# Self-attention of a transformer block on one core: value products issued for two key tiles at a time, with eight buffers for the exponentials instead of four

## The reference

```python
h = _layernorm(x, ln1_g, ln1_b)
x = _attention(h, h, sa_wq, sa_wk, sa_wv, sa_wo, sa_bo) + x
h = _layernorm(x, ln2_g, ln2_b)
x = _attention(h, cond_emb, ca_wq, ca_wk, ca_wv, ca_wo, ca_bo) + x
h = _layernorm(x, ln3_g, ln3_b)
...
# in _attention
attn = jnp.einsum('bihd,bjhd->bhij', q, k) * scale
attn = jax.nn.softmax(attn, axis=-1)
out = jnp.einsum('bhij,bjhd->bihd', attn, v).reshape(B, S, D_ATTN)
return out @ wo + bo
```

## Time and profile before

| | us |
|---|---|
| median of 3 runs (lowest, highest) | 1568.81 (1566.72, 1576.96) |
| span of the profiled execution | 1578.7 |
| TensorE busy | 1469.8 (93%) |
| VectorE busy | 979.5 (62%) |
| ScalarE busy | 858.7 (54%) |
| GpSimd busy | 923.3 (58%) |

### The profile page before, as it was taken

The page is one execution under the profiler, slowest core; times in us unless marked ns, Lnnn a source line. Parts: engine busy times, 40 slices in busy tenths (PEclk is TensorE's granted clock), DMA queues, the critical chain, the costliest instruction groups (busy, mean ns, idle before and its releaser), DMA issues.

```text
span 1578.7 us, 21167 instructions
## 1 busy us (share of the span) xinstructions
PE 1469.8 (93%) x5921; PEld 821.4 (52%) x5921; DVE 979.5 (62%) x1311; ACT 858.7 (54%) x1498; POOL 923.3 (58%) x513
## 2 busy tenths in 40 slices
PE   5589999999999999999999998689999999968998
PEld 3344555555555555555555543344555555426776
DVE  6457766766776676677667643536777777744333
ACT  4346565565655656565565643546666667535333
POOL 6026767757766775776677687436667777553000
PEclk9689999999999999999999998869999999979999
DMA  2000000000000000000000000200000000000000
GB/s 70 11 14 14 13 2 14 15 0 13 13 1 13 13 13 0 13 13 0 13 14 3 1 13 0 88 20 18 24 24 24 12 24 24 7 1 0 14 13 27
DMA packets 35737, 24.07 MB, mean 15 GB/s; under 512 B 2845, under 2 KB 35443, under 8 KB 35443
## 3 DMA queue, kind: packets, MB, share of 16 engines
q1 hardware_dynamic: 35699, 23.60, 4.9%
HBM read 21.23 MB, written 2.10 MB: 15 GB/s over the span
## 4 chain that ended last, share of the span: by engine, by line
PE 83%; ACT 6%; DVE 5%; POOL 3%; issue 2%; DMA 0%; ACTq 0%; SPq 0%; DVEq 0%; POOLq 0%
PE psum L582 20%; PE psum L502 13%; PE psum L569 11%; PE psum L546 9%; PE psum L570 8%; PE psum L655 5%; PE psum L591 4%; PE psum L644 3%; PE psum L606 2%; PE psum L608 2%; PE psum L607 2%; ACT probs L950 2%; PE psum L550 1%; PE psum L443 1%; PE psum L529 1%
## 5 line engine op out<-in xcount | busy, mean ns | idle before, releaser
L1083 POOL TENSOR_TENSOR acc<-acc,probs 128x1024 f32<-128x1024 f32 x192 | 458.2, 2386 | 184.3 <-ACT probs L950 175.1
L950 ACT ACTIVATE probs<-psum 128x512 f32<-128x512 f32 (+1 forms) x640 | 368.1, 594 | 256.9 <-PE psum L570 234.5
L767 DVE TENSOR_REDUCE m_part<-psum 128x1 f32<-128x512 f32 x512 | 344.9, 687 | 113.0 <-PE psum L546 108.7
L582 PE MATMUL psum<-probs,val 128*64 128x512 f32 (+1 forms) x1280 | 340.8, 620 | 0.2 <-ACT probs L950 0.2
L784 DVE RECIPROCAL recip<-psum 128x512 f32<-128x512 f32 x64 | 214.9, 3358 | 79.0 <-PE psum L591 79.0
L1083 POOL TENSOR_TENSOR acc<-probs 128x1024 f32<-128x1024 f32 (+1 forms) x64 | 152.7, 2386 | 120.1 <-ACT probs L950 71.0
L569 PE MATMUL psum<-qq,self_keys_hh 128*128 128x512 f32 x512 | 219.3, 428 | 2.2 <-ACT probs L950 2.1
L546 PE MATMUL psum<-self_keys_hh,qq 128*128 128x512 f32 x512 | 210.5, 431 | 6.1 <-DVE qq L761 2.8
L570 PE MATMUL psum<-qm,self_keys_lm 128*128 128x512 f32 x512 | 202.9, 396 | 0.0
L569 PEld LDWEIGHTS psum<-qq,self_keys_hh 128*128 128x128 f32 x512 | 96.7, 189 | 121.5 <-ACT probs L950 56.6
L546 PEld LDWEIGHTS psum<-self_keys_hh,qq 128*128 128x128 f32 x512 | 96.1, 190 | 117.5 <-DVE m_part L767 60.6
(11 more groups left out here) (122 smaller groups left out, 2165.5 us busy)
## 6 DMA issues: line engine op xcount, KB each, us to landing
w_raw<-in_L_xattn_ff_w SPq DMA_DIRECT2D x3, 1024.0 KB, 6.8
x_in<-in_x SPq DMA_DIRECT2D x4, 512.0 KB, 4.2
w_raw<-in_L_xattn_sa_wq SPq DMA_DIRECT2D x16, 128.0 KB, 2.1
w_raw<-in_L_xattn_sa_wk SPq DMA_DIRECT2D x16, 128.0 KB, 2.3
w_raw<-in_L_xattn_sa_wv SPq DMA_DIRECT2D x16, 128.0 KB, 2.4
qm<-m_rows SPq DMA_DIRECT2D x128, 2.0 KB
wo_raw<-in_L_xattn_sa_wo SPq DMA_DIRECT2D x16, 128.0 KB, 2.1
w_raw<-in_L_xattn_ca_wq SPq DMA_DIRECT2D x16, 128.0 KB, 2.3
```

What stands on the lines that cost most here:

```text
L582: mm = pe.matmul(psum[d, PV + half % plan.pv_banks, :], val[b][0:plan.ks, kt, d], probs[a % 4][0:plan.ks, h, :], start=(kt == 0), stop=(kt ...
L767: dve.tensor_reduce(m_part[:, half, h, t, kh:kh + 1], psum[:, PV + plan.pv_banks + a % plan.mx_banks, :], AX.X, ALU.max).then_inc(S["x_rea ...
L950: act.activation(probs[u % 4][0:plan.ks, h, :], psum[0:plan.ks, SC + h, :], ACT.Exp, scale=SCALE).then_inc(S["exp_done"], 1)
L1083: pool.tensor_tensor(total, last if kt == 1 else total, now, ALU.add).then_inc(S["acc_done"], 1)
```

## The change

The string for TensorE is written in another order; those of the other engines stay as they are. `P13- P14-`, `P2 P3`, `P4 P5`, `P6 P7`, `P8 P9` and `P10 P11` now stand next to each other, where another step stood between them before; `P15- P0 P1` stood together already, and `P12` stays alone. `P2`, `P4`, `P6` and `P8` move down to the place of the following product, `P13-` and `P10` move down by one step. The buffers `probs` become eight for the self-attention (four of them are used by the cross-attention, as before), and ScalarE's waits for a free buffer reach back eight units instead of four.

```diff
+PROBS = 8
...
-    "pe": "S0.0 S0.1 K0+ P13- S1.0 P14- S1.1 D1- K1+ S2.0 S2.1 P15- P0 P1 S3.0 Q0+ S3.1 S4.0 P2 S4.1 S5.0 "
+    "pe": "S0.0 S0.1 K0+ S1.0 P13- P14- S1.1 D1- K1+ S2.0 S2.1 P15- P0 P1 S3.0 Q0+ S3.1 S4.0 S4.1 S5.0 X0+ Q1+ "
...
+        self.probs = PROBS if own else 4
...
-        probs = [sb(f"probs{b}", [P, 2, HALF], F32, late) for b in range(4)]
+        probs = [sb(f"probs{b}", [P, 2, HALF], F32, late) for b in range(PROBS)]
...
-                                mm = pe.matmul(psum[d, PV + half % plan.pv_banks, :], val[b][0:plan.ks, kt, d], probs[a % 4][0:plan.ks, h, :],
+                                mm = pe.matmul(psum[d, PV + half % plan.pv_banks, :], val[b][0:plan.ks, kt, d], probs[a % plan.probs][0:plan.ks, h, :],
...
-                                after(act, S["pv_done"], plan.units * J + u - 3)
-                                pair, back = (J, u - 4) if u >= 4 else (J - 1, u - 4 + plan.units)
+                                after(act, S["pv_done"], plan.units * J + u - plan.probs + 1)
+                                pair, back = (J, u - plan.probs) if u >= plan.probs else (J - 1, u - plan.probs + plan.units)
                                 after(act, S["acc_done"], 2 * (plan.kt - 1) * pair + plan.added(back))
```

More of the change, by code:

```diff
@@ L944, in emit @@
                             if h == 0:
-                                after(act, S["pv_done"], plan.units * J + u - 3)
-                                pair, back = (J, u - 4) if u >= 4 else (J - 1, u - 4 + plan.units)
+                                after(act, S["pv_done"], plan.units * J + u - plan.probs + 1)
+                                pair, back = (J, u - plan.probs) if u >= plan.probs else (J - 1, u - plan.probs + plan.units)
                                 after(act, S["acc_done"], 2 * (plan.kt - 1) * pair + plan.added(back))
                             act.wait_ge(S["s_ready"], 2 * plan.units * J + 2 * u + h + 1)
-                            act.activation(probs[u % 4][0:plan.ks, h, :], psum[0:plan.ks, SC + h, :], ACT.Exp,
+                            act.activation(probs[u % plan.probs][0:plan.ks, h, :], psum[0:plan.ks, SC + h, :], ACT.Exp,
                                            scale=SCALE).then_inc(S["exp_done"], 1)
@@ L1074, in emit @@
                                 continue
-                            now, last = probs[u % 4][0:plan.ks], probs[(u - 1) % 4][0:plan.ks]
+                            now, last = probs[u % plan.probs][0:plan.ks], probs[(u - 1) % plan.probs][0:plan.ks]
                             total = acc[half][0:plan.ks]
```

## The result

The changed kernel takes 1593.15 us (median of 4 runs, 1590.89 to 1601.55) against 1570.01 us of the kernel before (1566.72 to 1576.96): ratio 1.014, 95% interval 1.0096 to 1.0183. It is slower, by 23 us in the medians; forecast were 21.

What follows compares the result with a forecast made beforehand. TensorE's own sequence was taken to bound the kernel; six moved products sum to +1.47 us per body, 22 us over fifteen bodies, less 1 for buffers, so 1568.8 + 21 = 1590 us, range 1568 to 1598.

Steps and rivals of the forecast that it cites:

- The bound: TensorE is busy throughout a self-attention body, so a body takes what its TensorE steps take, back to back.
- A join is worth 0.34 us: A lone product costs 1.20 us, each beyond the first in a group 0.86; changing the tiling mode drains TensorE.
- P2: Moved to P3: S4.1 waits 1.12 us for exponential S3.1, so nothing is saved; net +0.86 us per body.
- P6 and P8: Moved to P7 and P9: VectorE's reductions hold X12, X13, X24, X25; net +0.67 and +0.47 us per body.
- P4: Moved to P5: V1 waits for ScalarE's copy of V0, gaining 0.71 and costing 0.86; net +0.15 us per body.
- P10 and P13-: Each moves past one step, X29 or S1.0, and uncovers no wait; net -0.34 us each per body.
- The buffers: Eight buffers save 1 us (0 to 3), in the last body; ScalarE's 9.7 us of buffer waits lie in first and last.
- The sum: +1.47 us per body over fifteen bodies is 22, less 1 for the buffers: +21 us, giving 1590 us.
- The whole gain of the joins: Rival: no waits arise at P2, P4, P6, P8, so all six joins win 31 us, giving 1538; chance 0.09.
- VectorE catches up: Rival: P6 and P8 become plain joins, -0.35 us per body, -5 us, giving 1563; chance 0.22.
- The clock: Rival: TensorE's short pauses drop its clock to 1.2 GHz for 6 us per body, giving 1635; chance 0.04.
- slower by over 1%: Outcome above 1584.5 us: 0.55 from the forecast, with the clock rival 0.59.

Runs made afterwards that it cites:

- p10_p13_alone: Kernel before, four buffers, with only P10 moved down to P11 and P13- to P14-; 1569.09 us, ratio 0.9953 to the kernel before.
- four_joins: Kernel before, four buffers, with P13- P14- D1- together and D0 P10 P11 together (D are sums), X30+ before S14.0; 1551.48 us, ratio 0.9855.
- q_split: Changed kernel with the self-attention's copy of the second head of Q moved from ScalarE to VectorE; 1591.5 us, ratio 1.0112 to the kernel before.
- p2_alone: Kernel before with eight buffers and only P2 moved down to P3; 1592.78 us, ratio 1.0097 to the kernel before.
- buffers8: Kernel before with eight buffers instead of four, TensorE's order unchanged; 1575.67 us, ratio 0.9982 to the kernel before.
- order4: Changed kernel's order with four buffers instead of eight; 1592.64 us, ratio 1.0104 to the kernel before.
- p6_p8_alone: Kernel before with eight buffers, only P6 moved down to P7 and P8 down to P9; 1595.51 us, ratio 1.0109 to the kernel before.

## Why the prediction was right

**The bound.** That TensorE's own sequence is the time of a body held: every body length above follows from the starts of TensorE's steps.

**A join is worth 0.34 us.** Shown alone by p10_p13_alone (-0.69 for two) and by four_joins (-1.32 for four, two of them with sums instead of products). One rival is left for the cause. The products differ from their neighbours in two ways, 64 columns instead of 128 and plain float32 instead of float32r, and no run changes one of them alone. The trace speaks against the second: the four transposes `T1+` are plain float32 on all 128 columns, and in the changed kernel they and the `X` behind them take 642.19 to 642.85, 0.66 us. The transposes start 0.11 us apart, and 4 x 0.11 and 0.23 for the `X` make 0.67, so nothing comes on top.

```profile
642.19 0.60 PE L531 MATMUL psum<-ident,valT 128*128 128x128 f32 x4
642.54 0.47 PE L548 MATMUL psum<-self_keys_hh,qq 128*128 128x512 f32 x1
642.85 0.39 PE L571 MATMUL psum<-qq,self_keys_hh 128*128 128x512 f32 x1
```

So the 64 columns are the likely reason, as the prediction has it, and not a shown one.

**P2.** Forecast +0.86 per body, measured alone +0.84. The wait before `S4.1` was 1.14 us from start to start, forecast 1.12, and q_split shows that it is ScalarE's copying of `Q0` that sets it.

**P6 and P8.** Forecast +0.67 and +0.47, measured together +1.15. In the change, `X13` starts at 636.08 and `S7.1` 0.34 later, as the two rules taken from the earlier trace rows say; those two numbers (0.06 for the signal, 0.11 for the restart) carry all four places.

**P4.** Forecast +0.15, not run alone. What is left of the whole, 1.43 - 0.84 - 1.15 + 0.69 = +0.13, is its term. The trace of the change says the same: `V1` starts 0.62 us behind `X6` (628.24 to 628.86), forecast 0.63.

**P10 and P13-.** Forecast -0.68, measured -0.69.

**The buffers.** Right that they are worth nothing; the reason given for the first and last body was not. The prediction read the 9.7 us of the earlier trace rows as waits for a free buffer. With eight buffers the same waits are listed with the same lengths (2.5 us in the first body, 4.7 in two in the last), so they were waits for something else, put down to GpSimd by the table. Hence no microsecond came back in the last body.

**The sum.** Forecast +21, of which 22 by fifteen bodies; measured +1.43 x 15 = 21.4 by the same reckoning. The whole self-attention grew by 23.2 us. Of this the thirteen bodies in the middle have 18.5. The last one has 1.1, from its first scores to its last (39.43 to 40.51 us): the prediction took it as untouched by the order and 1 us shorter by the buffers, but `P2` is moved there too, and p2_alone has 40.30. The first two have 3.6, and how much of that is the change is open, as two kernels with the same order differ there by 1.5 (111.9 us before, 110.4 in buffers8).

That 1590 came so near to 1593.15 is in part luck. The 21 us were added to a median of 1568.8; beside the experiments the kernel before took 1577, and the same order (order4) was then 15 us slower and not 23. The body lengths, which don't depend on this, are what the sum can be held to.

**The rivals.** The whole gain of the joins fails at P2, P6 and P8, each for its own wait. That VectorE catches up fails by p6_p8_alone; its reductions at 0.60 us were not in the rows either, for three in 2.16 us are 0.72 each. The clock stays at 1.00 in the bodies with TensorE busy 54.05 of 56 us; the caution of the Trainium skill on short pauses (TensorE: Matmul & The Clock Gate, "A second HAM failure mode: psum-queue depth-cycling") isn't borne out by pauses of 0.2 to 1.0 us here.

The ratio is 1.014, slower by over 1%, to which the prediction gave a chance of 0.59.

## What to carry to other kernels

When an engine is busy all the time in an order written by hand, a step that is moved away must be replaced at its old place: ask of its follower when it may start at the earliest, and only the part of the step's cost up to there is won. Joining steps of one shape pays at the places where that start is not later; here two of six were such places, and looking for others of the same shape (the sums beside the products) gave four joins and 1.5%. Measure such changes by the distance between equal steps of the loop, which told 0.02 us of 55 apart while the total time scattered by 15; where totals must be compared, compare runs with the same mean clock.

## What the runs showed of the hardware

- Matmuls on 64 columns in plain float32 follow each other at 0.86 us per product of two heads; going from full-width matmuls to these and back costs 0.34 us more, for sums and products alike (`P13- P14- D1-` won two such costs, 6.87 to 6.15 us).
- A TensorE that waited pays 0.11 us more on its second matmul (0.34 us from start to start, and not 0.23), in the change as in the last body of the kernel before.
- A matmul that follows a product has the same 0.34 us to the next one without having waited (613.64 to 613.98 in the earlier trace rows).
- The table of waits can name a releaser that isn't one: the waits put down to GpSimd's additions stayed when the buffers they would free were doubled.
- The granted clock stayed at 1.00 (2.4 GHz) through the bodies, with pauses of 0.2 to 1.0 us in them (54.05 of 56 us busy). At the start of the cross-attention (30.78 of 40 us busy) it fell to 1.2 GHz, for stretches that differed between two profiles by 21 us.
